# Last epilogue of a two-layer adjacency kernel: partial sums seeded in PSUM, one fp32 product, statistics by squares

## The chip, the core and the metric

The kernel runs on one core of one Trainium2 chip. The metric is the device time of one execution in microseconds (us): lower is better. Three executions of the kernel before gave 796.47, 796.64 and 797.36 us, median 796.64 us.

## What is computed

Two graph layers over 4096 nodes with 256 features, each followed by a residual and a layer norm:

```python
def layer0(h, adj):
    h_neigh = (adj / (adj.sum(1, keepdims=True) + 1e-5)) @ h
    return relu(h_neigh @ W_neigh.T + b_neigh + h @ W_self.T + b_self)

def layer1(x, adj):
    d = where(adj.sum(1) > 0, adj.sum(1) ** -0.5, 0)
    return relu(((d[:, None] * adj * d[None, :]) @ x) @ W + b)

x = layernorm(x + layer0(x, adj))
x = layernorm(x + layer1(x, adj))
```

## The kernel before

All instruction streams are written out by hand, one per engine, with semaphores between them; no scheduler reorders them. Each engine takes its own instructions strictly in the order of the code.

Output rows are made in 8 blocks of 512 nodes (NB, IB). For a block, the transposed product with the adjacency is accumulated in PSUM (ps_main, two copies that take turns) as two feature halves f of 128 partitions by 512 columns. The 4096 contracted nodes come in 16 units (NU) of 256, loaded into a ring of four buffers (RING). To keep fp32 accuracy at the fast rate, every operand is split in two parts: ScalarE copies x to an fp32r part hi (split_hi, line 276), VectorE subtracts it to get lo (split_lo, line 432), and TensorE makes three products, hi by hi, hi by lo and lo by hi (line 770). The epilogue of a block (its product with the weights, then scale, bias, relu, residual and layer norm) is spread over the units of the next block.

The last block has no next block, and this is where the change is. TensorE stops the ordinary loop four units before its end (TAIL is 12) and goes over to last_epilogue, in which the last four units stand once for each column half h of 256 columns (HB):

```python
for f in range(FH):
    for u in range(TAIL, NU):
        half_unit(0, f, u)
half_unit(1, 0, TAIL)
half_unit(1, 0, TAIL + 1)
half_product(0, 0)
half_product(0, 1)
half_unit(1, 0, TAIL + 2)
half_unit(1, 0, TAIL + 3)
for u in range(TAIL, NU):
    half_unit(1, 1, u)
half_product(1, 0)
half_product(1, 1)
```

half_unit(h, f, u) (line 790) is six matmuls of 256 columns. For h = 0 it goes on adding to ps_main[1]. For h = 1 it writes ps_main[0], beginning afresh with start=True, so the sum of units 0 to 11 for these columns still stands in ps_main[1]. ScalarE's keep_partial(f) (line 378) copies it into SBUF (the xt buffer), and VectorE's add_partial(f) (line 630) adds the two and writes the whole sum to SBUF. There the sum is split again by stationary_hi_late and stationary_lo_late (lines 276 and 432).

half_product(h, k) (line 800) multiplies feature half k of the sums with the weights w1, in three fp32r matmuls for each row tile t of 128 rows: tiles 0 and 1 for h = 0, tiles 2 and 3 for h = 1. A row tile is complete after k = 1.

VectorE's rows(h) then does, for its two tiles, scale_product (line 462, out of PSUM), add_residual (line 479), bn_stats (line 638), bn_aggr (lines 649 and 650) and root_in (line 653). ScalarE's square_root(h) (line 387) takes the root, VectorE's scales(h) (lines 659 to 667) makes one Newton step and nmr, and ScalarE's normalise (line 391) writes the rows, save tile 2 of the last half, which VectorE writes (line 681). Output DMAs follow from SyncE and from ScalarE's queue.

In last_epilogue ScalarE's order is stationary_hi(0), stationary_hi(1), keep_partial(0), keep_partial(1), square_root(0), stationary_hi_late(0), stationary_hi_late(1), normalise(0, 0), normalise(0, 1), square_root(1), normalise(1, 3). stationary_hi(f) waits for half_done f + 1, that is for the last half_unit(0, f, u). Of the semaphores that the change touches, part_ready counts the kept partial sums, half_done the feature halves finished by TensorE, sth_ready and stl_ready the hi and lo parts, tile_done the finished row tiles.

Of the kernel before, what the change touches and what calls it, by code (L numbers as in the profile page):

```python
# [24 lines left out]
F = 256  # L25
P = 128
FH = F // P
# [20 lines left out]
def build(nc, x_nat, xt_in, adj_in, wn_in, bn_in, ws_in, bs_in, w1_in, b1_in, out):  # L48
# [6 lines left out]
    with ctx:  # L55
# [49 lines left out]
        warm_set = sem("warm_set")  # L105
        part_ready, whole_ready = sem("part_ready"), sem("whole_ready")
        x_full = [sem(f"x_full{s}") for s in range(2)]
# [51 lines left out]

        def partial(f):  # L160

            return xt[:, f, 0:HB]

        def whole(f):
            return xt[:, f, HB:IB]

# [106 lines left out]
        def _(act):  # L273
# [96 lines left out]
            def last_epilogue(epi):  # L370
# [5 lines left out]
                def keep_partial(f):  # L376
                    act.wait_ge(stl_ready, 2 * NB + f)
                    act.activation(partial(f), ps_main[1][:, f, HB:IB], ACT.Copy).then_inc(part_ready, 1)

                def stationary_hi_late(f):  # L380
                    act.wait_ge(whole_ready, f + 1)
                    split_hi(st_hi[:, f, HB:IB], whole(f)).then_inc(sth_ready, 1)

# [15 lines left out]
                stationary_hi_late(0)  # L399
                stationary_hi_late(1)  # L400
                normalise(0, 0)
                normalise(0, 1)
                square_root(1)
                normalise(1, TB - 1)
# [13 lines left out]
        def _(dve):  # L418
# [198 lines left out]
            def last_epilogue(epi):  # L617
# [8 lines left out]

                def add_partial(f):
                    dve.wait_ge(part_ready, f + 1)
                    dve.wait_ge(half_done, FH + f + 1)
                    dve.tensor_tensor(whole(f), ps_main[0][:, f, 0:HB], partial(f), ALU.add).then_inc(whole_ready, 1)  # L630

                def stationary_lo_late(f):
                    dve.wait_ge(sth_ready, n + 1 + FH + f)
                    split_lo(st_lo[:, f, HB:IB], whole(f), st_hi[:, f, HB:IB]).then_inc(stl_ready, 1)

# [3 lines left out]

                def rows(h):  # L640
                    t = h * HT
                    scale_product(layer, n, t)
                    scale_product(layer, n, t + 1)
                    add_residual(n, t)
                    add_residual(n, t + 1)
                    statistics(t)
                    statistics(t + 1)
                    linked()
                    dve.bn_aggr(mv[:, t, :], stats[:, t, :])
                    link(dve.bn_aggr(mv[:, t + 1, :], stats[:, t + 1, :]))  # L650
                    linked()
                    at = slice(t, t + HT)
                    dve.tensor_scalar(root_in[:, at], mv[:, at, 1], EPS_NORM, None, ALU.add).then_inc(root_ready, 1)

                def scales(h):
                    at = slice(h * HT, (h + 1) * HT)
                    r, q, a = inv_root[:, at], newton[:, at], root_in[:, at]
                    dve.wait_ge(root_taken, 2 * NB + h)
                    link(dve.reciprocal(r, root[:, at]))
                    linked()  # L660
                    link(dve.scalar_tensor_tensor(out=q, in0=a, scalar=-0.5, in1=r, op0=ALU.mult, op1=ALU.mult))
                    linked()
                    link(dve.tensor_tensor(q, q, r, ALU.mult))
                    linked()
                    link(dve.scalar_tensor_tensor(out=r, in0=q, scalar=1.5, in1=r, op0=ALU.add, op1=ALU.mult))
                    linked()
                    dve.scalar_tensor_tensor(out=nmr[:, at], in0=mv[:, at, 0], scalar=-1.0, in1=r,
                                             op0=ALU.mult, op1=ALU.mult).then_inc(norm_ready, 1)

                stationary_lo(0)  # L670
                stationary_lo(1)
                rows(0)
                add_partial(0)
                stationary_lo_late(0)
                scales(0)
                add_partial(1)
                stationary_lo_late(1)
                rows(1)
                scales(1)
# [9 lines left out]
        def _(pe):  # L689
# [88 lines left out]
            def last_epilogue(epi):  # L778
# [3 lines left out]
                def half_unit(h, f, u):  # L782
                    if (h, f) == (0, 0):
                        pe.wait_ge(z_ready, UJ * (u + 1))
                        pe.wait_ge(l_ready, g0 + (u + 1))
                    for q in range(UJ):
                        jt = u * UJ + q
                        cols = slice(q * IB + h * HB, q * IB + (h + 1) * HB)
                        for i, (part, mov) in enumerate(((0, hi), (0, lo), (1, hi))):
                            last = pe.matmul(ps_main[1 - h][:, f, 0:HB], stationary(1, part, jt, f),  # L790
                                             mov[:, slot(u), cols], start=(h == 1 and jt == TAIL * UJ and i == 0),
                                             stop=(jt == JT - 1 and i == 2))
# [3 lines left out]
                def half_product(h, k):  # L796
                    pe.wait_ge(stl_ready, n + 1 + h * FH + k)
                    for t in range(h * HT, (h + 1) * HT):
# [4 lines left out]
                        if k == FH - 1:  # L803
                            last.then_inc(tile_done, 1)

                for f in range(FH):
                    for u in range(TAIL, NU):
# [9 lines left out]
                half_product(1, 0)  # L817
                half_product(1, 1)

# [36 lines left out]
```

## Time and profile before

| | us |
|---|---|
| median of 3 runs | 796.64 (796.47 to 797.36) |
| the profiled execution, its own time | 796.24 |
| span of its records | 794.5 |
| TensorE matmul busy | 782.8 (99%) |
| VectorE busy | 579.2 (73%) |
| ScalarE busy | 388.8 (49%) |
| last_epilogue on TensorE begins | 771.39 |
| last matmul begins | 787.46 |
| last DMAs issued | 791.97 and 792.16 |

The span runs from the first to the last record; the profiled execution's own time is 1.74 us longer than it. In the row forms used here, a timeline row gives start, duration, engine (PE is TensorE's matmul, PEld its weight load, DVE is VectorE, ACT is ScalarE), the source line, the operation, out<-in and the shapes, and in brackets the idle time before it with what ended it. A row with x2 or more merges consecutive instructions that overlap in part. xt_sb, st_hi and st_lo are SBUF buffers; ps_main and ps_epi are in PSUM.

### The profile page before, as it was taken

The numbers are of one execution on the slowest core, as the hardware profiler recorded it, in microseconds if no ns is written. First come the engines' busy times: TensorE is split into PE (matmuls) and PEld (weight loads), VectorE is DVE, ScalarE is ACT, GpSimd is POOL, SyncE is SP. The second block draws the span as 40 slices with busy tenths as digits, with TensorE's granted clock in tenths as the row PEclk, the third lists the DMA queues.
The fourth block names the chain that finished last, engine by engine and source line by source line (L and its number), as shares of the span: only waits on it lengthen the run. The fifth ranks groups of instructions, "written<-read, shape, count | busy, mean of one in ns | idle before, by whom it ended". The sixth has DMA issues, their size and how long they took to land.

```text
span 794.5 us, 11181 instructions
## 1 busy us (share of the span) xinstructions
PE 782.8 (99%) x3759; PEld 655.9 (83%) x3759; DVE 579.2 (73%) x878; ACT 388.8 (49%) x534; POOL 0.3 (0%) x6
## 2 busy tenths in 40 slices
PE   8999999999999999999999999999999999999996
PEld 5788888888888888888888888888888888888885
DVE  5999989899898998989966554554555455554644
ACT  4554635546355463453644545355444535444452
POOL 0000000000000000000000000000000000000000
PEclk9999999999999999999999999999999999999999
DMA  8966665755646556465574655757575565757540
GB/s 319 310 241 208 198 229 168 232 179 178 244 158 216 202 166 241 158 233 185 186 235 162 213 200 189 237 181 235 167 247 170 188 235 177 237 168 245 177 159 27
DMA packets 54747, 160.93 MB, mean 203 GB/s; under 512 B 5056, under 2 KB 18752, under 8 KB 54720
## 3 DMA queue, kind: packets, MB, share of 16 engines
q1 hardware_dynamic: 46224, 152.06, 57.0%
q10 hardware_dynamic: 8496, 8.52, 3.2%
q8 instruction: 15, 0.25, 0.1%
q14 instruction: 12, 0.10, 0.0%
HBM read 152.17 MB, written 8.39 MB: 202 GB/s over the span
## 4 chain that ended last, share of the span: by engine, by line
PE 93%; DVE 5%; DMA 1%; ACT 0%; SPq 0%; issue 0%; ACTq 0%
PE ps_main L770 83%; PE ps_epi L695 8%; DVE lo L432 2%; DVE acc L610 1%; DMA raw<-adj_t 1%; PE ps_epi L716 1%; DVE xs L432 1%; PE ps_main L790 1%; ACT hi L276 0%; DVE st_lo L432 0%; PE ps_epi L800 0%; DVE stats L638 0%; DVE tt L479 0%; DVE tt L462 0%; DVE xt_sb L630 0%
## 5 line engine op out<-in xcount | busy, mean ns | idle before, releaser
L276 ACT ACTIVATE hi<-raw 128x1024 fp32r<-128x1024 f32 x254 | 269.2, 1061 | 338.3 <-PE ps_main L770 327.7
L432 DVE TENSOR_TENSOR lo<-raw,hi 128x1024 fp32r<-128x1024 f32 x254 | 310.2, 1221 | 137.8 <-ACT hi L276 137.7
L770 PE MATMUL ps_main<-hi,xs 128*128 128x512 f32 x1120 | 359.9, 391 | 1.9 <-DVE lo L432 1.9
L770 PE MATMUL ps_main<-hi,zs 128*128 128x512 f32 x880 | 278.1, 390 | 0.0
L770 PEld LDWEIGHTS ps_main<-hi,xs 128*128 128x128 f32 x1120 | 210.5, 188 | 46.9 <-issue 4.3
L770 PE MATMUL ps_main<-lo,xs 128*128 128x512 f32 x560 | 218.6, 390 | 0.0
L770 PEld LDWEIGHTS ps_main<-hi,zs 128*128 128x128 f32 x880 | 165.4, 188 | 33.6
L770 PE MATMUL ps_main<-lo,zs 128*128 128x512 f32 x440 | 171.6, 390 | 0.0
L610 DVE TENSOR_TENSOR acc<-acc,raw 128x1024 f32<-128x1024 f32 x112 | 136.1, 1215 | 0.0
L770 PEld LDWEIGHTS ps_main<-lo,xs 128*128 128x128 f32 x560 | 105.4, 188 | 19.3
L770 PEld LDWEIGHTS ps_main<-lo,zs 128*128 128x128 f32 x440 | 82.8, 188 | 16.0
L462 DVE SCALAR_TENSOR_TENSOR tt<-ps_epi,d_cur,bias 128x256 f32<-128x256 f32 x32 | 15.3, 483 | 41.0 <-PE ps_epi L695 38.6
L301 ACT ACTIVATE tt<-tt,nmr,inv_root 128x256 f32<-128x256 f32 x60 | 32.5, 588 | 4.7 <-DVE nmr L516 4.7
L432 DVE TENSOR_TENSOR st_lo<-ps_main,st_hi 128x1024 fp32r<-128x1024 f32 (+1 forms) x17 | 19.2, 1130 | 17.4 <-ACT st_hi L276 17.4
L276 ACT ACTIVATE st_hi<-ps_main 128x1024 fp32r<-128x1024 f32 (+1 forms) x17 | 16.2, 953 | 29.9 <-PE ps_main L770 25.0
L295 ACT ACTIVATE ps_epi<-tt,nmean 128x256 f32<-128x256 f32 x60 | 27.6, 459 | 0.0
L479 DVE SCALAR_TENSOR_TENSOR tt<-tt,res 128x256 f32<-128x256 f32 x64 | 26.6, 418 | 0.2
L695 PE MATMUL ps_epi<-ws_sb,st_hi 128*128 128x256 f32 x128 | 24.2, 282 | 0.0
L695 PE MATMUL ps_epi<-wn_sb,st_hi 128*128 128x256 f32 x128 | 24.2, 282 | 0.0
L695 PEld LDWEIGHTS ps_epi<-wn_sb,st_hi 128*128 128x128 f32 x128 | 22.0, 190 | 2.5
L695 PEld LDWEIGHTS ps_epi<-ws_sb,st_hi 128*128 128x128 f32 x128 | 22.0, 190 | 2.5
L695 PE MATMUL ps_epi<-xs,st_hi 128*128 128x256 f32 x112 | 21.2, 282 | 0.0
(92 smaller groups left out, 369.2 us busy)
## 6 DMA issues: line engine op xcount, KB each, us to landing
raw<-adj_t SPq DMA_DIRECT2D x255, 512.0 KB, 3.3
res<-x_nat SPq DMA_DIRECT2D x11, 512.0 KB, 6.0
xt_sb<-xt SPq DMA_DIRECT2D x8, 512.0 KB, 5.2
x_scratch<-tt ACTq DMA_DIRECT2D x8, 512.0 KB, 5.8
res<-x_scratch SPq DMA_DIRECT2D x8, 512.0 KB, 6.4
out<-tt ACTq DMA_DIRECT2D x7, 512.0 KB, 6.8
tt<-x_nat SPq DMA_DIRECT2D x4, 512.0 KB, 5.5
raw<-adj_t SPq DMA_DIRECT2D x2, 256.0 KB, 4.3
```

Source lines behind the costliest of these rows:

```text
L276: return act.activation(dst, src, ACT.Copy)
L295: act.activation(ps_epi[:, t, 0:F], tt[:, t, :], ACT.Square, bias=nmean[:, t:t + 1], accum_out=squares[:, t:t + 1]).then_inc(squares_ready, 1)
L301: act.activation(tt[:, t, :], tt[:, t, :], ACT.Identity, bias=nmr[:, t:t + 1], scale=rstd[:, t:t + 1]).then_inc(x1_ready, 1)
L432: return dve.tensor_tensor(dst, src, hi_part.bitcast(f32), ALU.subtract)
L462: ins = dve.scalar_tensor_tensor(out=tt[:, t, :], in0=ps_epi[:, t, 0:F], scalar=(rdeg, d_cur)[layer][:, t:t + 1], in1=(bias0, bias1)[layer ...
L479: link(dve.scalar_tensor_tensor(out=tt[:, t, :], in0=tt[:, t, :], scalar=0.0, in1=res[:, t, :], op0=ALU.max, op1=ALU.add, accum_out=sums[: ...
L610: dve.tensor_tensor(a, a, raw[:, slot(u), :], ALU.add).then_inc(acc_done, 1)
L695: last = pe.matmul(ps, st[:, k, rows], weight(part, k), start=(k == 0 and q == 0), stop=(k == FH - 1 and q == 2))
L716: last = pe.matmul(ps_epi[:, TB - 1, t:t + 1], acc[:, parity, t * P:(t + 1) * P], ones[:, :], start=True, stop=True)
L770: last = pe.matmul(ps[:, f, :], stationary(layer, part, jt, f), mov[:, slot(u), cols], start=(jt == 0 and i == 0), stop=(jt == JT - 1 and ...
L790: last = pe.matmul(ps_main[1 - h][:, f, 0:HB], stationary(1, part, jt, f), mov[:, slot(u), cols], start=(h == 1 and jt == TAIL * UJ and i ...
```

## The change

Four edits, all in last_epilogue:

- keep_partial(f) writes the kept sums of units 0 to 11 into ps_main[0] instead of SBUF, and TensorE's h = 1 matmuls add onto them (start=False throughout). TensorE now waits for part_ready at the first h = 1 matmul of each feature half. add_partial is gone.
- For feature half 0 the split (stationary_hi_late(0), stationary_lo_late(0)) reads PSUM directly.
- For feature half 1 of column half 1 there is no split. ScalarE copies the sum to SBUF as fp32 (stationary_whole, behind both normalise instructions of the first half), and TensorE multiplies it in plain fp32 with the unsplit w1, one matmul for each row tile (whole_product).
- The statistics of tiles 2 and 3 come as in the other blocks: sum from add_residual's accumulator, mean by VectorE, squares by ScalarE with an accumulator (square_late, written to res). For tiles 0 and 1 one small VectorE instruction (nmean) is added, and nmr is made from it.

```diff
--- before.py
+++ after.py
@@ -103,7 +103,7 @@
         raw_head = sem("raw_head")
         x_first_full = [sem(f"x_first_full{i}") for i in range(3)]
         warm_set = sem("warm_set")
-        part_ready, whole_ready = sem("part_ready"), sem("whole_ready")
+        part_ready, late_ready = sem("part_ready"), sem("late_ready")
         x_full = [sem(f"x_full{s}") for s in range(2)]
         wn_full, ws_full, w1_full, bias_full = sem("wn_full"), sem("ws_full"), sem("w1_full"), sem("bias_full")
         xt_full, res_full = sem("xt_full"), sem("res_full")
@@ -157,12 +157,12 @@
                 return xs[:, t:t + 1]
             return zs[:, bass.ds(e * TB + t, 1)]
 
-        def partial(f):
-
-            return xt[:, f, 0:HB]
-
-        def whole(f):
-            return xt[:, f, HB:IB]
+        def late_columns(f):
+
+            return ps_main[0][:, f, 0:HB]
+
+        late_rows = xt[:, FH - 1, HB:IB]
+        w1_raw = xt[:, FH - 1, 0:F]
 
         def moving_weight(layer, part, k):
             if layer == 0:
@@ -375,11 +375,20 @@
 
                 def keep_partial(f):
                     act.wait_ge(stl_ready, 2 * NB + f)
-                    act.activation(partial(f), ps_main[1][:, f, HB:IB], ACT.Copy).then_inc(part_ready, 1)
+                    act.activation(late_columns(f), ps_main[1][:, f, HB:IB], ACT.Copy).then_inc(part_ready, 1)
 
                 def stationary_hi_late(f):
-                    act.wait_ge(whole_ready, f + 1)
-                    split_hi(st_hi[:, f, HB:IB], whole(f)).then_inc(sth_ready, 1)
+                    act.wait_ge(half_done, FH + f + 1)
+                    split_hi(st_hi[:, f, HB:IB], late_columns(f)).then_inc(sth_ready, 1)
+
+                def stationary_whole():
+                    act.wait_ge(half_done, 2 * FH)
+                    act.activation(late_rows, late_columns(FH - 1), ACT.Copy).then_inc(late_ready, 1)
+
+                def square_late(t):
+                    act.wait_ge(mean_ready, (2 * NB - 1) * 2 + t - HT + 1)
+                    act.activation(res[:, t, :], tt[:, t, :], ACT.Square, bias=nmean[:, t:t + 1],
+                                   accum_out=squares[:, t:t + 1]).then_inc(squares_ready, 1)
 
                 def square_root(h):
                     act.wait_ge(root_ready, 2 * NB + h)
@@ -397,9 +406,11 @@
                 keep_partial(1)
                 square_root(0)
                 stationary_hi_late(0)
-                stationary_hi_late(1)
                 normalise(0, 0)
                 normalise(0, 1)
+                stationary_whole()
+                square_late(HT)
+                square_late(HT + 1)
                 square_root(1)
                 normalise(1, TB - 1)
                 act.wait_ge(x1_ready, (2 * NB - 1) * TB + HT + 1)
@@ -624,33 +635,38 @@
                     dve.wait_ge(sth_ready, n + 1 + f)
                     split_lo(st_lo[:, f, 0:HB], ps_main[1][:, f, 0:HB], st_hi[:, f, 0:HB]).then_inc(stl_ready, 1)
 
-                def add_partial(f):
-                    dve.wait_ge(part_ready, f + 1)
-                    dve.wait_ge(half_done, FH + f + 1)
-                    dve.tensor_tensor(whole(f), ps_main[0][:, f, 0:HB], partial(f), ALU.add).then_inc(whole_ready, 1)
-
                 def stationary_lo_late(f):
                     dve.wait_ge(sth_ready, n + 1 + FH + f)
-                    split_lo(st_lo[:, f, HB:IB], whole(f), st_hi[:, f, HB:IB]).then_inc(stl_ready, 1)
+                    split_lo(st_lo[:, f, HB:IB], late_columns(f), st_hi[:, f, HB:IB]).then_inc(stl_ready, 1)
 
                 def statistics(t):
                     linked(but=1 if t % HT == 0 else 0)
                     link(dve.bn_stats(stats[:, t, :], tt[:, t, :]))
 
-                def rows(h):
-                    t = h * HT
+                def early_rows():
+                    scale_product(layer, n, 0)
+                    scale_product(layer, n, 1)
+                    add_residual(n, 0)
+                    add_residual(n, 1)
+                    statistics(0)
+                    statistics(1)
+                    linked()
+                    dve.bn_aggr(mv[:, 0, :], stats[:, 0, :])
+                    link(dve.bn_aggr(mv[:, 1, :], stats[:, 1, :]))
+                    linked()
+                    dve.tensor_scalar(root_in[:, 0:HT], mv[:, 0:HT, 1], EPS_NORM, None, ALU.add).then_inc(root_ready, 1)
+                    dve.tensor_scalar(nmean[:, 0:HT], mv[:, 0:HT, 0], -1.0, None, ALU.mult)
+
+                def late_row_tile(t):
                     scale_product(layer, n, t)
-                    scale_product(layer, n, t + 1)
                     add_residual(n, t)
-                    add_residual(n, t + 1)
-                    statistics(t)
-                    statistics(t + 1)
-                    linked()
-                    dve.bn_aggr(mv[:, t, :], stats[:, t, :])
-                    link(dve.bn_aggr(mv[:, t + 1, :], stats[:, t + 1, :]))
-                    linked()
-                    at = slice(t, t + HT)
-                    dve.tensor_scalar(root_in[:, at], mv[:, at, 1], EPS_NORM, None, ALU.add).then_inc(root_ready, 1)
+                    linked()
+                    dve.tensor_scalar(nmean[:, t:t + 1], sums[:, t:t + 1], -1.0 / F, None, ALU.mult).then_inc(mean_ready, 1)
+
+                def late_root_argument():
+                    dve.wait_ge(squares_ready, (2 * NB - 1) * TB + HT)
+                    dve.tensor_scalar(root_in[:, HT:TB], squares[:, HT:TB], 1.0 / F, EPS_NORM, ALU.mult, ALU.add)\
+                       .then_inc(root_ready, 1)
 
                 def scales(h):
                     at = slice(h * HT, (h + 1) * HT)
@@ -664,18 +680,16 @@
                     linked()
                     link(dve.scalar_tensor_tensor(out=r, in0=q, scalar=1.5, in1=r, op0=ALU.add, op1=ALU.mult))
                     linked()
-                    dve.scalar_tensor_tensor(out=nmr[:, at], in0=mv[:, at, 0], scalar=-1.0, in1=r,
-                                             op0=ALU.mult, op1=ALU.mult).then_inc(norm_ready, 1)
+                    dve.tensor_tensor(nmr[:, at], nmean[:, at], r, ALU.mult).then_inc(norm_ready, 1)
 
                 stationary_lo(0)
                 stationary_lo(1)
-                rows(0)
-                add_partial(0)
+                early_rows()
                 stationary_lo_late(0)
                 scales(0)
-                add_partial(1)
-                stationary_lo_late(1)
-                rows(1)
+                late_row_tile(HT)
+                late_row_tile(HT + 1)
+                late_root_argument()
                 scales(1)
                 dve.wait_ge(norm_ready, 2 * NB + 1)
                 dve.tensor_scalar(tt[:, HT, :], tt[:, HT, :], rstd[:, HT:HT + 1], nmr[:, HT:HT + 1],
@@ -783,12 +797,14 @@
                     if (h, f) == (0, 0):
                         pe.wait_ge(z_ready, UJ * (u + 1))
                         pe.wait_ge(l_ready, g0 + (u + 1))
+                    if h == 1 and u == TAIL:
+                        pe.wait_ge(part_ready, f + 1)
                     for q in range(UJ):
                         jt = u * UJ + q
                         cols = slice(q * IB + h * HB, q * IB + (h + 1) * HB)
                         for i, (part, mov) in enumerate(((0, hi), (0, lo), (1, hi))):
                             last = pe.matmul(ps_main[1 - h][:, f, 0:HB], stationary(1, part, jt, f),
-                                             mov[:, slot(u), cols], start=(h == 1 and jt == TAIL * UJ and i == 0),
+                                             mov[:, slot(u), cols], start=False, skip_group_check=(h == 1),
                                              stop=(jt == JT - 1 and i == 2))
                     if u == NU - 1:
                         last.then_inc(half_done, 1)
@@ -802,6 +818,12 @@
                                              start=(k == 0 and q == 0), stop=(k == FH - 1 and q == 2))
                         if k == FH - 1:
                             last.then_inc(tile_done, 1)
+
+                def whole_product():
+                    pe.wait_ge(late_ready, 1)
+                    for t in range(HT, TB):
+                        pe.matmul(ps_epi[:, t, 0:F], late_rows[:, (t - HT) * P:(t - HT + 1) * P], w1_raw,
+                                  start=False, stop=True).then_inc(tile_done, 1)
 
                 for f in range(FH):
                     for u in range(TAIL, NU):
@@ -815,7 +837,7 @@
                 for u in range(TAIL, NU):
                     half_unit(1, 1, u)
                 half_product(1, 0)
-                half_product(1, 1)
+                whole_product()
 
             layers(pe, one_block, last_epilogue)
 
```

The order on two engines, by the kernel's own instruction lists. First ScalarE from the start of last_epilogue, before (all of it up to the output DMA):

```order
L276 ACTIVATE st_hi<-ps_main 128x256 [waits half_done] x2
L378 ACTIVATE xt_sb<-ps_main 128x256 [waits stl_ready] x2
L387 ACTIVATE root<-root_in 128x2 [waits root_ready]
L276 ACTIVATE st_hi<-xt_sb 128x256 [waits whole_ready] x2
L391 ACTIVATE tt<-tt,nmr,inv_root 128x256 [waits norm_ready] x2
L387 ACTIVATE root<-root_in 128x2 [waits root_ready]
L391 ACTIVATE tt<-tt,nmr,inv_root 128x256 [waits norm_ready]
```

The same place on ScalarE in the changed kernel:

```order
L276 ACTIVATE st_hi<-ps_main 128x256 [waits half_done] x2
L378 ACTIVATE ps_main<-ps_main 128x256 [waits stl_ready] x2
L396 ACTIVATE root<-root_in 128x2 [waits root_ready]
L276 ACTIVATE st_hi<-ps_main 128x256 [waits half_done]
L400 ACTIVATE tt<-tt,nmr,inv_root 128x256 [waits norm_ready] x2
L386 ACTIVATE xt_sb<-ps_main 128x256 [waits half_done]
L390 ACTIVATE res,squares<-tt,nmean 128x256 [waits mean_ready] x2
L396 ACTIVATE root<-root_in 128x2 [waits root_ready]
L400 ACTIVATE tt<-tt,nmr,inv_root 128x256 [waits norm_ready]
```

Both st_hi instructions still stand ahead of both partial copies; the second late st_hi is gone, and the copy at line 386 stands behind both normalise instructions.

TensorE at the seam between column half 0 and column half 1 in the changed kernel (hi, lo are the adjacency parts, xs and zs the feature parts):

```order
L806 MATMUL ps_main<-lo,xs 128x256
L806 MATMUL ps_main<-hi,xs 128x256
L806 MATMUL ps_main<-hi,zs 128x256 [waits part_ready]
L806 MATMUL ps_main<-lo,zs 128x256
L806 MATMUL ps_main<-hi,zs 128x256 x2
```

The third row is the first matmul of column half 1; it had no wait before and now waits for ScalarE's first partial copy. Everything behind it on TensorE, the weight product of tiles 0 and 1 included, is queued behind that wait.

VectorE from the scale product of tile 2 to the root argument. Before:

```order
L462 SCALAR_TENSOR_TENSOR tt<-ps_epi,d_cur,bias 128x256 [waits tile_done] x2
L479 SCALAR_TENSOR_TENSOR tt,sums<-tt,res 128x256 [waits tile_read] x2
L638 BN_STATS stats<-tt 128x6 [waits dve_chain] x2
L649 BN_AGGR mv<-stats 128x2 [waits dve_chain]
L650 BN_AGGR mv<-stats 128x2
L653 TENSOR_SCALAR root_in<-mv 128x2 [waits dve_chain]
```

Changed:

```order
L473 SCALAR_TENSOR_TENSOR tt<-ps_epi,d_cur,bias 128x256 [waits tile_done]
L490 SCALAR_TENSOR_TENSOR tt,sums<-tt,res 128x256 [waits tile_read]
L664 TENSOR_SCALAR nmean<-sums 128x1 [waits dve_chain]
L473 SCALAR_TENSOR_TENSOR tt<-ps_epi,d_cur,bias 128x256 [waits tile_done]
L490 SCALAR_TENSOR_TENSOR tt,sums<-tt,res 128x256 [waits tile_read]
L664 TENSOR_SCALAR nmean<-sums 128x1 [waits dve_chain]
L668 TENSOR_SCALAR root_in<-squares 128x2 [waits squares_ready]
```

The tiles now go one after the other, each with two waits on VectorE's own results, and root_in waits for ScalarE's squares.

## Rows read from the trace of the kernel before

**Rows 1.** The chain of waits, 771 us to the end: start us, us, what

```profile
774.12 5.27 PE ps_main L790 x42
780.51 0.54 DVE tt L462 x2
...
783.26 0.44 DVE xt_sb L630
...
785.38 0.44 DVE xt_sb L630
...
786.76 0.64 PE ps_epi L800 x3
...
787.43 0.88 DVE tt L462 x2
...
790.11 0.18 DVE root_in L653
```

**Rows 2.** Timeline, seam of the column halves

```profile
775.52 0.42 DVE L432 TENSOR_TENSOR st_lo<-ps_main,st_hi 128x256 fp32r<-128x256 f32 x1 [1.47 <-ACT st_hi L276]
...
777.79 0.28 PE L790 MATMUL ps_main<-hi,zs 128*128 128x256 f32 x1
...
777.99 0.38 ACT L276 ACTIVATE st_hi<-ps_main 128x256 fp32r<-128x256 f32 x1 [2.50 <-PE ps_main L790]
...
778.27 0.38 ACT L378 ACTIVATE xt_sb<-ps_main 128x256 f32<-128x256 f32 x1
```

**Rows 3.** Timeline, TensorE taking up work after an idle stretch

```profile
774.12 0.36 PE L790 MATMUL ps_main<-hi,xs 128*128 128x256 f32 x1 [0.41 <-DVE lo L432]
774.31 0.28 PE L790 MATMUL ps_main<-lo,xs 128*128 128x256 f32 x1
```

**Rows 4.** Instructions grouped by line and form, ScalarE, whole span: count, busy us, mean ns

```profile
L295 ACT ACTIVATE ps_epi<-tt,nmean 128x256 f32<-128x256 f32 x60 | 27.6, 459 | 0.0
...
L306 ACT ACTIVATE zs<-tt,d_cur 128x256 f32 x24 | 11.3, 494 | 0.0
...
L276 ACT ACTIVATE st_hi<-ps_main 128x256 fp32r<-128x256 f32 x2 | 0.8, 384 | 4.9 <-PE ps_main L790 4.9
L378 ACT ACTIVATE xt_sb<-ps_main 128x256 f32<-128x256 f32 x2 | 0.8, 381 | 0.2 <-DVE st_lo L432 0.2
```

**Rows 5.** Timeline, from the first half's statistics to the late split

```profile
783.18 0.17 DVE L653 TENSOR_SCALAR root_in<-mv 128x2 f32<-128x2 f32 x1
783.26 0.42 DVE L630 TENSOR_TENSOR xt_sb<-ps_main,xt_sb 128x256 f32<-128x256 f32 x1
...
783.39 0.20 ACT L387 ACTIVATE root<-root_in 128x2 f32<-128x2 f32 x1 [4.14 <-DVE root_in L653]
...
784.17 0.43 DVE L432 TENSOR_TENSOR st_lo<-xt_sb,st_hi 128x256 fp32r<-128x256 f32 x1 [0.48 <-ACT st_hi L276]
...
784.87 0.28 PE L790 MATMUL ps_main<-hi,xs 128*128 128x256 f32 x1
...
785.30 0.16 DVE L667 SCALAR_TENSOR_TENSOR nmr<-mv,inv_root 128x2 f32<-128x2 f32 x1
...
786.16 1.08 ACT L391 ACTIVATE tt<-tt,nmr,inv_root 128x256 f32<-128x256 f32 x2
786.28 0.43 DVE L432 TENSOR_TENSOR st_lo<-xt_sb,st_hi 128x256 fp32r<-128x256 f32 x1 [0.48 <-ACT st_hi L276]
```

**Rows 6.** Unsplit fp32 matmuls of the first two units: ns min/median/max

```profile
L753 PE MATMUL ps_main<-raw,acc x16: 592/592/976, 5.0 to 11.8; 128*128 128x512 f32 x16
```

**Rows 7.** Timeline of TensorE's weight loads, same stretch

```profile
10.12 0.19 PEld L753 LDWEIGHTS ps_main<-raw,acc 128*128 128x128 f32 x1 [0.24 <-issue]
```

**Rows 8.** Timeline, end of a square by ScalarE with its accumulator read, an earlier block

```profile
759.02 0.46 ACT L295 ACTIVATE ps_epi<-tt,nmean 128x256 f32<-128x256 f32 x1
...
759.42 0.19 ACT L295 ACTIVATION_READ_ACCUMULATOR ps_epi<-tt,nmean 128x1 f32 x1
```

**Rows 9.** Engines by stretch: PE, PEld, DVE, ACT, POOL busy, granted clock, DMA share, GB/s

```profile
783.00:787.00 4.00, 3.10 (x26) 2.90 (x26) 2.57 (x12) 1.79 (x5) 0.00 (x0) 1.00 0.00 0
```

## The prediction

> **What bounds the kernel now.** I read the chain of waits first, since all four edits lie in the last 20 us. Up to 771 us it is TensorE with its main loop, which the change leaves alone. From 774.12 it runs through 42 matmuls of the last units and the weight product of tiles 0 and 1, goes over to VectorE at 780.51, and from there alternates in short steps: root_in, add_partial(0) at 783.26, add_partial(1) at 785.38, its split, and TensorE again only at 786.76 for the last weight product [rows 1]. The timeline agrees that TensorE is not the limit at the end: its last sum is under way at 784.87 and done about 785.2, but VectorE's order puts the Newton step of the first half ahead of add_partial(1) [rows 5]. After 787.43 a chain of VectorE and ScalarE leads to root_in at 790.11 [rows 1]; 4.2 us of the 794.5 us span follow its end. So a microsecond anywhere on TensorE between 778 and 781 is paid in full, as VectorE's first half starts that much later, and the edits have to be walked through in time. That the average share of TensorE is 99% says nothing here.
>
> **The seam (loss).** TensorE goes from column half 0 to column half 1 at 777.79 without a pause [rows 2]. Now that matmul waits for keep_partial(0). The copy's own input was long ready: VectorE's st_lo(0) ended at 775.94. But ScalarE takes its instructions in order, and stationary_hi(1) stands ahead; it waits for the end of the very half unit that TensorE has just issued. It ran from 777.99, and the copy from 778.27 [rows 2]. Two rows bound the copy. PSUM to SBUF takes 0.381 us; a destination in PSUM cost less for the squares (0.459) than a destination in SBUF for a one-pointer copy (0.494), a difference of 0.035 [rows 4]. I take 0.381 - 0.035 = 0.35, ending 778.62; the ends are 0.31 (the saving counted twice) and 0.46 (no PSUM-to-PSUM row exists, so the slowest of these to PSUM). With 0.05 from semaphore to start (st_lo ends 786.71, TensorE starts 786.76 [rows 1, 5]) TensorE resumes at 778.67. After an idle stretch the second matmul comes 0.19 after the first [rows 3], where 42 in 5.27 us [rows 1] give 0.12: 0.07 more. Shift: 778.67 - 777.79 + 0.07 = **+0.95**, with ends of +0.9 and +1.1. What is queued behind it: two half units, both weight products of the first half, and so all of VectorE's early rows. The second wait, for part_ready 2 at the first unit of f = 1, is free: that copy ends about 1 us after the seam, five microseconds before it is wanted.
>
> **First half to the late copy (gain).** Everything up to the end of root_in (783.35 [rows 5]) moves to 784.30. ScalarE's root, 783.39 before, runs 784.34 to 784.54. add_partial(0) with its 0.42 us is gone: stationary_hi_late(0) reads PSUM, whose sum is complete at about 783.3, so it starts right behind the root, 0.1 before its end as neighbours on ScalarE do [rows 2], takes 0.38 [rows 4] and ends 784.82. The added nmean instruction (0.17, like root_in) lies in that gap on VectorE and costs nothing; without the gap it would cost 0.1 to 0.17. st_lo starts at 784.85; from its start to the end of nmr it was 785.46 - 784.17 = 1.29 [rows 5], so nmr ends at 786.14, 0.68 later than before instead of 0.95.
>
> add_partial(1), stationary_hi_late(1) and stationary_lo_late(1) are removed, 0.44 + 0.45 + 0.48 us from 785.38 to 786.76 [rows 1, 5]. In their place stands one copy, but behind both normalise instructions in ScalarE's order. These took 1.08 together [rows 5] and now run 786.18 to 787.26. The sum that the copy needs is complete at 785.15 + 0.95 = 786.10, so it is ScalarE's queue that it waits for, not TensorE. Copy 787.16 to 787.54 (0.38 [rows 4]), TensorE starts at 787.59 instead of 786.76: **+0.83**. The three removed instructions are nearly worth the stall, but the two normalises now lie in front.
>
> **The fp32 product.** Before, tile 2 took three matmuls and VectorE started 787.43 - 786.76 = 0.67 after the first [rows 1]. The trace has unsplit fp32 matmuls in the first two units: 16 records for 8 matmuls of 512 columns, one record each 0.43 us (0.19 busy, 0.24 idle on the weight side [rows 7]), 0.592 long [rows 6]. So a record holds 0.43 us of streaming and 0.16 of latency; with 256 columns the two records need 0.215 each, 0.43 for a tile, plus 0.16, plus 0.10 for taking up work and 0.04 to VectorE: 0.73, **+0.06**. Lower end 0 (no start penalty), upper end +0.33, if the two records do not overlap and each takes its 0.38 in full. Tile 3 comes 0.43 later and is ready long before VectorE wants it.
>
> **The statistics.** Before, from the start of the scale product to the end of root_in: 790.11 + 0.18 - 787.43 = 2.86 [rows 1]. Now, from zero: scale 0.48, residual 0.51 to 0.93, mean 0.95 to 1.11; scale of tile 3 1.02 to 1.50, residual 1.53 to 1.95, mean 1.97 to 2.13; square on ScalarE from 2.17. A square to PSUM ends with its accumulator read 759.42 + 0.19 - 759.02 = 0.59 after its start [rows 8], and with an SBUF destination 0.035 more [rows 4], at 2.79; root_in 2.83 to 3.00. **+0.15**, ends 0 and +0.3: the two bn_stats and bn_aggr, 1.1 us side by side, are traded for waits in series. Tile 2's square is hidden behind tile 3's rows.
>
> The Trainium skill, "ScalarE: Activation LUTs", section "Step-by-step: what each stage is for", says that ScalarE reaches PSUM faster than SBUF, which speaks against the move of the squares to res. The case's 0.459 and 0.494 agree [rows 4]. Its section "What ACT_TABLE_LOAD costs" prices a one-pointer ACTIVATE at 280 ns + 0.833 ns per element, 493 ns at 256 elements, whatever the destination; by that the sum would be the same within 0.04 us.
>
> **Sum.** 0.83 + 0.06 + 0.15 = **+1.04 us**; behind root_in nothing changes. The profiled execution took 796.24 us, 0.40 under the median; on the median this makes 796.64 + 1.04 = **797.7 us**, 0.13% more. A measurement of this kernel can tell about 0.2%, 1.6 us, from no change, so I forecast no measurable difference, leaning slower.
>
> **Rivals.**
> (a) *The stall does not take place* or is off the path. Then the late product starts at 786.76 + 0.83 - 0.95 = 786.64, the sum is -0.12 + 0.06 + 0.15 = +0.09, and the time 796.7 us. It would need the copy to be done by 777.79. For it: its input is ready at 775.94. Against it: ScalarE's order in the code, and the row at 778.27 [rows 2]. 6%.
> (b) *TensorE's clock falls* at the seam. The kernel now has two idle stretches, 0.9 us at the seam and about 1 us before the fp32 product. If the granted clock halves from the seam on, the 66 matmuls from there to the end of half_product(1, 0) take 0.24 instead of 0.12: +7.9 us, time about 805. It decides from a fall ahead of half_product(1, 0), as 14 matmuls at half speed already make +1.6. Against it: the stretch from 783 to 787 had 0.9 us of idle TensorE and a granted clock of 1.00 [rows 9]. 4%. The Trainium skill, "TensorE: Matmul & The Clock Gate", section "What's actually happening", names idleness as what brings the gate back to 1.2 GHz; the trace shows no fall after a gap of this size.
> (c) *The fp32 records do not overlap*: +0.33 in place of +0.06, sum +1.31, time 798.0. For it: pipelining of the two records of one matmul is seen only at 512 columns. Against it: a weight load of 0.19 [rows 7] still fits under 0.215. 8%.
> The forecast has the remaining 82%.
>
> **Numbers.** The term ends give +0.7 (0.9 at the seam and nothing for product and statistics) to +1.8. The three runs shown spread over 0.9 us, so a median may lie 0.4 off. Low end 796.5, which takes in (a); high end 798.8, which takes in (c) and leaves out (b). Slower by over 0.2% means above 798.23: (b) with 4%, and 10% from the upper ends of forecast and (c), 0.14. Faster by over 0.2% means below 795.05; nothing in the ledger gives it, 0.02. Within: 0.84.
>
> **What would show it.** A TensorE gap of about 0.9 us ahead of the first h = 1 matmul, ended by ScalarE's copy; the first scale product 0.95 us later against the seam; the copy at line 386 starting at the end of the second normalise with no idle time; two fp32 matmuls of some 0.43 us each; 3.0 us from the scale product of tile 2 to root_in. I would be wrong if the first h = 1 matmul followed without a gap, if the copy were released by TensorE, or if the granted clock left 1.00 before the last product.

## Result and the profile after

The changed kernel took **797.87 us** (median of 22 runs, 797.45 to 798.48). The kernel before took 796.62 us in 22 runs beside it. The ratio is 1.0014, with a 95% interval of 1.0008 to 1.0020: 1.25 us slower, clear of noise over so many runs and under the 0.2% of the prediction's bound.

| | before | changed |
|---|---|---|
| span of the profiled execution, us | 794.5 | 795.7 |
| TensorE matmul busy, us | 782.8 | 782.9 |
| first matmul after the last adjacency unit's lo part | 774.12 | 774.21 |
| scale product of tile 0 begins | 780.51 | 781.61 |
| last product begins | 786.76 | 787.73 |
| scale product of tile 2 begins | 787.43 | 788.47 |
| last root_in ends | 790.29 | 791.50 |
| ScalarE's last normalise begins | 791.53 | 792.74 |

TensorE's busy time is the same; what grew is the last 20 us. From the first to the last row of the table's times it was 17.41 us before and is 18.53 now, 1.12 more. The other 0.09 us was lost ahead of 774, where the code is the same: the first adjacency load on the chain takes 7.79 us in this profile and took 7.71 before.

The chain of waits of the changed kernel over that stretch (start us, us, what) answers to [rows 1]:

```profile
774.21 3.84 PE ps_main L806 x30
778.06 0.02 issue
778.08 0.38 ACT st_hi L276
778.46 0.28 ACT ps_main L378
778.75 0.04 issue
778.79 1.70 PE ps_main L806 x12
...
786.32 1.09 ACT tt L400 x2
787.41 0.28 ACT xt_sb L386
787.68 0.04 issue
787.73 0.71 PE ps_epi L825 x2
...
791.32 0.18 DVE root_in L668
```

Two pieces are new on it. At 778.08 the chain leaves TensorE for ScalarE's st_hi and then the partial copy, where before it ran on through 42 matmuls. At 786.32 it goes through both normalise instructions before the late copy; before, they were not on the chain.

The timeline at the seam answers to [rows 2]:

```profile
778.08 0.38 ACT L276 ACTIVATE st_hi<-ps_main 128x256 fp32r<-128x256 f32 x1 [2.49 <-PE ps_main L806]
778.36 0.38 ACT L378 ACTIVATE ps_main<-ps_main 128x256 f32<-128x256 f32 x1
```

```profile
777.76 0.28 PE L806 MATMUL ps_main<-hi,xs 128*128 128x256 f32 x1
778.79 0.39 PE L806 MATMUL ps_main<-hi,zs 128*128 128x256 f32 x1 [0.75 <-ACT ps_main L378]
779.01 0.28 PE L806 MATMUL ps_main<-lo,zs 128*128 128x256 f32 x1
```

The first matmul of column half 1 starts 1.03 us after the last of half 0, where the step is 0.12 otherwise, and the next one needs 0.22: the seam costs 1.01 us. What the copy itself waits for, VectorE's low part of feature half 0, had been done for over 2 us (it ended at 776.04); ScalarE had been waiting (2.49 us in the brackets) for the input of the instruction in front of it.

The timeline around the late copy and the fp32 product:

```profile
786.32 1.09 ACT L400 ACTIVATE tt<-tt,nmr,inv_root 128x256 f32<-128x256 f32 x2 [1.35 <-DVE nmr L683]
...
786.69 0.28 PE L816 MATMUL ps_epi<-xs,st_lo 128*128 128x256 f32 x1
...
787.31 0.36 ACT L386 ACTIVATE xt_sb<-ps_main 128x256 f32<-128x256 f32 x1
...
787.73 1.13 PE L825 MATMUL ps_epi<-xt_sb 128*128 128x256 f32 x4 [0.76 <-ACT xt_sb L386]
788.47 0.48 DVE L473 SCALAR_TENSOR_TENSOR tt<-ps_epi,d_cur,bias 128x256 f32<-128x256 f32 x1 [2.19 <-PE ps_epi L825]
```

The copy begins inside the last 0.1 us of the second normalise, without idle time on ScalarE; TensorE stands 0.76 us. The two fp32 matmuls are four records.

### The profile page after: what moved, and what is told of

The parts are those of the page before. It is cut to its first block, busy times and chain, and to the rows that moved or that the text cites. A ratio compares the mean times of both kernels' runs of the same rounds, so it can differ in the third digit from the quotient of the medians.

```text
span 795.7 us, 11175 instructions
## 1 busy us (share of the span) xinstructions
PE 782.9 (98%) x3757; PEld 655.5 (82%) x3757; DVE 577.8 (73%) x874; ACT 389.6 (49%) x538; POOL 0.3 (0%) x6
## 4 chain that ended last, share of the span: by engine, by line
PE 92%; DVE 5%; DMA 1%; ACT 1%; SPq 0%; issue 0%; ACTq 0%
PE ps_main L784 83%; PE ps_epi L709 8%; DVE lo L443 2%; DVE acc L621 1%; DMA raw<-adj_t 1%; PE ps_epi L730 1%; DVE xs L443 1%; PE ps_main L806 1%; ACT hi L276 0%; ACT tt L400 0%; DVE tt L490 0%; DVE st_lo L443 0%; DVE tt L473 0%; PE ps_epi L816 0%; DVE stats L644 0%
```

## The experiments

Eight kernels, 11 timed runs each. The kernel before, beside them, took 796.63 us (33 runs) with each group of four. The head of the kernel varies: the first matmul after the last adjacency unit's lo part begins between 774.12 and 774.43 us in nine of the ten profiles, and at 775.28 in that of e3. So the last column gives the tail inside each profile: from that matmul to the start of ScalarE's last normalise.

| | median us | ratio to before (95%) | tail us |
|---|---|---|---|
| before | 796.62 | | 17.41 |
| changed | 797.87 | 1.0014 (1.0008 to 1.0020) | 18.53 |
| e1_seam | 796.68 | 1.0002 (0.9993 to 1.0011) | 17.53 |
| e2_late_copy | 796.48 | 0.9999 (0.9990 to 1.0008) | 17.53 |
| e3_both | 795.86 | 0.9990 (0.9981 to 0.9999) | 16.52 |
| e4_both_bn_stats | 795.36 | 0.9984 (0.9975 to 0.9993) | 16.39 |
| e5_both_bn_split | 795.87 | 0.9992 (0.9983 to 1.0001) | 16.78 |
| e6_mixed_stats | 795.20 | 0.9981 (0.9972 to 0.9990) | 16.15 |
| e7_wait_only | 797.59 | 1.0014 (1.0005 to 1.0023) | 18.41 |
| e8_paired_squares | 795.40 | 0.9987 (0.9978 to 0.9996) | 16.31 |

Each tail is that of one profiled execution. Stretches with the same code repeat closely: from the tail's start to the first record of the fp32 product it is 11.59 us in each of e3, e4, e6 and e8. The medians follow the tails less closely: e1 and e2 each shorten the tail by 1.00 us, and their medians lie 1.19 and 1.39 us under that of the changed kernel. What is left over lies ahead of the tail, where no edit was made, and its cause stays open. Kernels that are less than 0.4 us apart are therefore compared by their tails.

### e1_seam: the partial copy ahead of the high part

```diff
                 stationary_hi(0)
-                stationary_hi(1)
                 keep_partial(0)
+                stationary_hi(1)
                 keep_partial(1)
```

> The changed kernel with one swap on ScalarE: keep_partial(0) ahead of stationary_hi(1). Theory (the seam is paid through in-order ScalarE): the copy runs at about 776.1, the first matmul of column half 1 follows the last of half 0 without the 0.75 us idle stretch and the 0.10 us of taking up work, everything behind moves by 1.0 us, the time is about 796.9 us. Rival (the end is set by ScalarE's queue at the late copy alone, and the seam is slack): the gap at the seam goes, but the fp32 product still starts 9.7 us after the last matmul of half 0 as before, time 797.9 us.

Measured: 796.68 us, tail 17.53. ScalarE's and TensorE's timelines:

```profile
776.14 0.37 ACT L378 ACTIVATE ps_main<-ps_main 128x256 f32<-128x256 f32 x1 [0.49 <-DVE st_lo L443]
778.14 0.38 ACT L276 ACTIVATE st_hi<-ps_main 128x256 fp32r<-128x256 f32 x1 [1.64 <-PE ps_main L806]
```

```profile
777.82 0.28 PE L806 MATMUL ps_main<-hi,xs 128*128 128x256 f32 x1
777.94 0.28 PE L806 MATMUL ps_main<-hi,zs 128*128 128x256 f32 x1
```

The copy now runs as soon as VectorE's low part is there, TensorE goes over the seam with its ordinary step of 0.12, and the tail is 1.00 us shorter, all of it. The product begins 12.51 us after the tail's start against 13.52 in the changed kernel, and 8.96 us after the last matmul of half 0 against 9.97. The rival (slack at the seam) is refuted.

### e7_wait_only: the wait alone, in the kernel before

```diff
+                    if h == 1 and u == TAIL:
+                        pe.wait_ge(part_ready, f + 1)
                     for q in range(UJ):
```

> The kernel before with one line more: TensorE waits for part_ready f + 1 at the first matmul of each feature half of column half 1, nothing else changed (the sums still go through SBUF). Theory: the wait alone costs the 0.75 us gap and the 0.10 us of taking up work, 1.0 us in all from seam to seam, and all of it reaches the end, as VectorE's early rows start later: about 797.6 us. Rival (the kernel before has slack behind the seam): under 0.3 us, 796.9 us.

Measured: 797.59 us, tail 18.41, 1.00 longer than before. TensorE's timeline:

```profile
777.98 0.28 PE L792 MATMUL ps_main<-hi,xs 128*128 128x256 f32 x1
779.00 0.39 PE L792 MATMUL ps_main<-hi,zs 128*128 128x256 f32 x1 [0.75 <-ACT xt_sb L378]
```

One wait, added to a kernel otherwise untouched, makes the same gap of 0.75 us and costs what the swap of e1 gives back. Nothing is slack behind the seam. It also splits the result: the change is this wait (1.00) and 0.12 for all else together, which is what remained in e1's tail over the kernel before. That 0.12 is a balance: a second wait of 1.00 us lies in it (e2, below), and without both waits the change shortens the tail by 0.89 (e3).

### e2_late_copy: the late copy ahead of the normalises

```diff
+                stationary_whole()
                 normalise(0, 0)
                 normalise(0, 1)
-                stationary_whole()
```

> The changed kernel with stationary_whole ahead of both normalise instructions on ScalarE, the seam untouched. Theory: the copy is then released by TensorE's last sum at about 786.2, TensorE goes from half_product(1, 0) to the fp32 product at 786.8 without a gap, VectorE's scale product of tile 2 comes about 1.0 us earlier, time about 796.9 us. Rival (the end is set by the seam alone, the late copy being no limit): no change, 797.9 us.

Measured: 796.48 us, tail 17.53, again 1.00 less than in the changed kernel:

```profile
786.28 0.38 ACT L386 ACTIVATE xt_sb<-ps_main 128x256 f32<-128x256 f32 x1 [1.32 <-PE ps_main L806]
...
786.56 1.08 ACT L400 ACTIVATE tt<-tt,nmr,inv_root 128x256 f32<-128x256 f32 x2
...
786.68 0.28 PE L816 MATMUL ps_epi<-xs,st_lo 128*128 128x256 f32 x1
...
786.80 1.05 PE L825 MATMUL ps_epi<-xt_sb 128*128 128x256 f32 x4
...
787.46 0.48 DVE L473 SCALAR_TENSOR_TENSOR tt<-ps_epi,d_cur,bias 128x256 f32<-128x256 f32 x1 [1.18 <-PE ps_epi L825]
```

The copy is now released by TensorE's own last sum and hidden behind half_product(1, 0). TensorE goes on at 786.80 without a gap; so it also saves the time of taking up work, and VectorE starts 0.66 after the first fp32 record, 0.74 in the changed kernel. The normalises shift by 0.24 us, and nobody waits for them.

### e3_both: do the two gains add?

The edit is those of e1 and e2.

> Both swaps together. Theory: the two delays lie one behind the other on one chain, so the gains add, 1.0 + 1.0 us: the fp32 product about 1.9 us earlier than in the changed kernel, time about 795.9 us, 0.7 under the kernel before. Rival (both waits cover the same stretch): the pair gives no more than one of them, 796.9 us.

Measured: 795.86 us, tail 16.52: 2.01 less than the changed kernel's and 0.89 less than that of the kernel before. The gains add in full. The profiled execution itself took 796.53, because its tail begins only at 775.28. That microsecond (1.07 us) comes from the head, where its code is that of the changed kernel: the first load on the chain lands 0.45 us later than in the changed kernel's profile (8.24 us after its issue against 7.79), and ScalarE's copy of the transposed x starts at 36.75 against 35.43. This is why the tails are compared, and not the spans.

With both swaps the chain runs on TensorE to the end of the products:

```profile
775.28 5.27 PE ps_main L806 x42
780.55 1.44 PE ps_epi L816 x12
781.99 4.32 PE ps_main L806 x36
786.31 0.72 PE ps_epi L816 x6
787.03 0.47 PE ps_epi L825 x2
```

### e4_both_bn_stats: bn_stats for the late tiles

Taken from e3: the function of the early tiles serves both halves, and the squares go.

```diff
-                late_row_tile(HT)
-                late_row_tile(HT + 1)
-                late_root_argument()
+                rows(HT)
...
-                square_late(HT)
-                square_late(HT + 1)
```

> Both swaps, and the statistics of tiles 2 and 3 by bn_stats and bn_aggr side by side, as in the kernel before, in place of ScalarE's squares. Theory: from the start of the scale product of tile 2 to the end of root_in 2.86 us in place of 3.02, time 0.15 to 0.2 us under both swaps alone, 795.7 us. Rival (squares on ScalarE relieve VectorE and pay): 0.2 us or more above it.

Measured: 795.36 us, tail 16.39, 0.13 less than e3. From the start of tile 2's scale product to the end of root_in it is 786.52 to 789.42, 2.90 us, against 3.04 in e3. The gain is small, but it is against the rival, by which bn_stats would have been slower. The medians differ by 0.50, more than the tails; the remainder lies ahead of the tail and is not explained by this edit.

### e8_paired_squares: was it the squares or the series?

```diff
+                scale_product(layer, n, HT)
+                scale_product(layer, n, HT + 1)
                 late_row_tile(HT)
                 late_row_tile(HT + 1)
```

(against e3; late_row_tile loses its own scale_product)

> Both swaps; ScalarE still makes the squares of both late tiles, but VectorE does both scale products first, then residual and mean of tile 2, residual and mean of tile 3. Theory (the extra time of the changed statistics lies in taking the tiles one after the other, not in the square): 2.8 us from the scale product of tile 2 to the end of root_in, 0.25 us less than with the tiles in series, about 795.6 us. Rival (the square and its accumulator read are the price): no change against the series, 795.85 us.

Measured: 795.40 us, tail 16.31, 0.21 less than e3 and 0.08 less than with bn_stats:

```profile
786.59 0.92 DVE L473 SCALAR_TENSOR_TENSOR tt<-ps_epi,d_cur,bias 128x256 f32<-128x256 f32 x2 [1.18 <-PE ps_epi L826]
...
787.43 0.41 DVE L490 SCALAR_TENSOR_TENSOR tt<-tt,res 128x256 f32<-128x256 f32 x1
...
788.60 0.51 ACT L390 ACTIVATE res<-tt,nmean 128x256 f32<-128x256 f32 x1
789.02 0.19 ACT L390 ACTIVATION_READ_ACCUMULATOR res<-tt,nmean 128x1 f32 x1
789.24 0.17 DVE L667 TENSOR_SCALAR root_in<-squares 128x2 f32<-128x2 f32 x1 [0.67 <-ACT res L390]
```

From the start of tile 2's scale product to the end of root_in it is 2.83 us (2.8 expected), against 3.04 in e3 and 2.90 in e4. Two scale products that do not wait for each other take 0.92 together. In series each takes 0.48 and its residual can start only at its end. So the squares were no worse than bn_stats; what cost 0.21 us was to put the second scale product behind the first tile's residual and mean.

### e6_mixed_stats: one tile on each engine

```diff
+                scale_product(layer, n, HT)
+                scale_product(layer, n, HT + 1)
+                add_residual(n, HT)
+                add_residual(n, HT + 1)
...
+                link(dve.bn_stats(stats[:, HT, :], tt[:, HT, :]))
...
-                square_late(HT)
                 square_late(HT + 1)
```

(against e3; tile 3's mean comes before tile 2's bn_stats, and root_in is written in two columns)

> Both swaps; of the late tiles both scale products and both residuals go first, then tile 3's statistics by ScalarE's square, tile 2's by bn_stats on VectorE at the same time. Theory (the price of the squares was that they stood in series behind VectorE's chain): 2.6 us from the scale product of tile 2 to the end of root_in, as against 3.04 with squares and 2.90 with bn_stats; 0.3 us under bn_stats, about 795.1 us. Rival (the hand-over to ScalarE costs more than it saves): equal to bn_stats or slower, 795.4 us or more.

Measured: **795.20 us**, tail 16.15, the fastest of the study:

```profile
788.09 0.42 DVE L695 BATCH_NORM_STATS2 stats<-tt 128x6 f32<-128x256 f32 x1
788.21 0.51 ACT L390 ACTIVATE res<-tt,nmean 128x256 f32<-128x256 f32 x1 [1.64 <-DVE nmean L694]
788.54 0.18 DVE L697 BATCH_NORM_AGGREGATE mv<-stats 128x2 f32<-128x6 f32 x1
788.62 0.19 ACT L390 ACTIVATION_READ_ACCUMULATOR res<-tt,nmean 128x1 f32 x1
...
788.89 0.14 DVE L702 TENSOR_SCALAR root_in<-squares 128x1 f32<-128x1 f32 x1
```

ScalarE's square and VectorE's bn_stats run beside each other; from 786.39 to 789.03 it is 2.64 us, where 2.6 was expected. Its interval lies below one, 0.9972 to 0.9990. Against e4 (tail 0.24 shorter, median 0.16 lower) and e8 (0.16 and 0.20) the order rests on the tails.

### e5_both_bn_split: what the unsplit fp32 product is worth

Taken from e4: in place of the copy and the fp32 product, feature half 1 is split from PSUM and multiplied in three fp32r matmuls for each tile.

```diff
-                stationary_whole()
+                stationary_hi_late(1)
...
                 stationary_lo_late(0)
+                stationary_lo_late(1)
                 scales(0)
...
-                whole_product()
+                half_product(1, 1)
```

> Both swaps and bn_stats, and feature half 1 of column half 1 is split into hi and lo again (both read from PSUM) and multiplied in three fp32r matmuls for each tile, in place of the copy and the unsplit fp32 product. Theory: the last sum stands at about 785.3; ScalarE's hi 0.38, VectorE's lo 0.43 and 0.05 each for the hand-overs put the product at 786.25 instead of 786.02, three matmuls then bring tile 2 0.63 us later as against 0.50 measured for fp32 without a gap in front: 0.3 us more than with bn_stats alone, about 795.7 us. In this place VectorE also has the Newton step queued behind the lo part. Rival (the unsplit product is worth the larger part of a microsecond, or nothing, because half_product(1, 0) covers the split): 796.1 us or more, or 795.4 us.

Measured: 795.87 us, tail 16.78, 0.39 more than e4 and more than the 0.3 expected. The timeline:

```profile
785.43 0.38 ACT L276 ACTIVATE st_hi<-ps_main 128x256 fp32r<-128x256 f32 x1 [1.32 <-PE ps_main L804]
...
785.85 0.42 DVE L441 TENSOR_TENSOR st_lo<-ps_main,st_hi 128x256 fp32r<-128x256 f32 x1 [1.28 <-ACT st_hi L276]
...
786.33 0.50 PE L814 MATMUL ps_epi<-xs,st_hi 128*128 128x256 f32 x2 [0.22 <-DVE st_lo L441]
...
786.96 0.16 DVE L682 TENSOR_TENSOR nmr<-nmean,inv_root 128x2 f32<-128x2 f32 x1
787.04 0.87 DVE L471 SCALAR_TENSOR_TENSOR tt<-ps_epi,d_cur,bias 128x256 f32<-128x256 f32 x2
```

The second hand-over leaves a TensorE gap of 0.22 us, and the product begins 11.97 us after the tail's start, 0.38 later than in e4. The Newton step, queued behind the low part, adds little: tile 2 could have been read some 0.67 us after the product's start [rows 1], at 787.00, and VectorE started at 787.04. So the unsplit product, with the split that it does without, is a real gain of about 0.4 us, which the changed kernel did not show because its operand came late.

The run tells one thing more. It has the same products and the same kind of statistics as the kernel before; it differs from it in the sums made directly in PSUM and in the order on ScalarE and VectorE that goes with them. Its tail is 0.63 shorter. Of the 1.02 us between the kernel before and e4, 0.63 belong to the direct sums with that order and 0.39 to the unsplit product.

## Why the prediction was right

**Seam.** Predicted: ScalarE's order makes TensorE wait, +0.95. Measured 1.01. The mechanism stands by e1 and e7, each of which moved the tail by 1.00. The size was 0.06 short in two places. The copy from PSUM to PSUM took 0.374 on average, where I had taken 0.035 off the 0.381 [rows 4] for the destination; that saving, read from instructions that read SBUF, did not come where the source is PSUM. And the second matmul after the gap came 0.22 later, not 0.19. The Trainium skill, "ScalarE: Activation LUTs", section "Step-by-step: what each stage is for", calls PSUM the faster destination; the trace agrees for the squares (0.459 to PSUM, 0.508 to SBUF) and does not for copies out of PSUM (0.374 to PSUM; 0.381 and 0.361 to SBUF).

**First half to the late copy.** Predicted the product 0.83 later than before; measured 0.97, of which 0.09 is the later start of the tail: 0.88. The 0.05 is the seam's. The late copy was held by ScalarE's two normalises and not by TensorE, as predicted: the row at 787.31 has no idle time before it, and e2 took this away. The added nmean on VectorE was hidden. So was the second wait of TensorE, for part_ready 2: that copy ended 3.9 us before it was wanted, not five as written.

**fp32 product.** Predicted 0.73 to VectorE's start, measured 0.74, +0.07. The two records overlap: four records take 1.13 us after a gap and 1.05 without one, though each is 0.38 long or longer. So rival (c) is refuted, but not by the time. Its +0.33 is summed wrongly: two records of 0.38, with 0.10 and 0.04, make 0.90 us, +0.23 over 0.67, and a sum of +1.21, which is 797.85 us. That is even nearer to the measured 797.87 than the forecast's 797.7; only the rows tell the two apart.

**Statistics.** Predicted 3.00 us, measured 791.50 - 788.47 = 3.03, against 2.86: +0.17. The cause given, waits in series, is what e8 shows. The surplus lies in VectorE's steps ahead of the square of tile 3, which began 2.22 us after the scale product where 2.17 was forecast. The square with its accumulator read took 0.60, under the 0.62 forecast, although its ACTIVATE took 0.508 against 0.494.

**Sum.** 0.88 + 0.07 + 0.17 = 1.12 in the tail against 1.04 predicted, plus 0.09 ahead of it: the 1.21 by which the last normalise is later. The median moved by 1.25. All three terms were right in mechanism, and each was forecast slightly too small. The 0.09 in the head was not forecast and is of the size by which heads differ among the profiles.

**Rivals.** (a) is refuted by the gap itself; but the state that it describes is that of e1, and its price held there: +0.09 forecast, 0.12 more in the tail than before (796.7 us forecast, 796.68 measured, closer than a median can be trusted here). (b): the granted clock did not leave 1.00 before the last product was done. The stretches with the seam's gap and up to the late product read (PE, PEld, DVE, ACT, POOL busy, clock, DMA share, GB/s):

```profile
775.00:779.00 4.00, 3.25 (x27) 3.05 (x26) 0.85 (x2) 1.09 (x4) 0.00 (x0) 1.00 0.02 4
779.00:783.00 4.00, 4.00 (x35) 4.00 (x35) 1.39 (x5) 0.32 (x1) 0.00 (x0) 1.00 0.00 0
783.00:787.00 4.00, 3.97 (x34) 3.76 (x32) 2.57 (x14) 1.16 (x4) 0.00 (x0) 1.00 0.00 0
```

From 787.70 to 789.00, with the fp32 product behind its own gap of 0.76 us, it is 1.00 as well; it falls only after 793, when TensorE has no work left. TensorE stayed at 2.4 GHz after idling 0.75 us, as it had in the kernel before after 0.9 us ([rows 9], and 1.00 from 787.00 to 787.70).

The bound of 0.2% on what can be told apart was too coarse: with 22 runs on each side the interval is 0.12% wide, and a change of 0.14% is clear of noise.

## What to carry to other kernels

When a change puts a new wait on the busiest engine, look at the instruction that stands in front of the releasing one in its in-order queue, not only at when the releaser's input is ready: here a copy that could have run 2 us early stood behind one that waited for the very engine it held up. Such an edit can be sound and still lose. The direct sums in PSUM and the unsplit product lost 1.25 us in the order given, and with two swaps on ScalarE, paired tiles and statistics split over two engines they gained 1.4 us (795.20 against 796.63, e6). Where short dependent steps make a tail, try two tiles side by side, and their statistics on two engines: here the first gave 0.21 us (e8) and the second 0.16 more (e6), read from the tails.

## What the runs showed of the hardware

- ScalarE copies of 128x256 out of PSUM take about the same time to PSUM (0.374 us) as to SBUF (0.361 to 0.381), while squares read from SBUF take 0.459 us to PSUM and 0.508 to SBUF.
- TensorE pays some 0.1 us for taking up work after a gap of 0.75 us: the second 256-column matmul follows after 0.22 instead of 0.12. VectorE's start after the first fp32 record moved from 0.66 to 0.74 with a gap in front.
- An unsplit fp32 matmul of 256 columns is two records of 0.379 us (0.484 the first after a gap) that overlap; with no gap in front VectorE can read the result 0.66 us after the start, about as soon as after three fp32r matmuls with a gap in front (0.67 [rows 1]).
